# Layer entries reordered, an f16 projection in the fourth layer, and the adjacency's row sums on ScalarE

## The reference

```python
def reference(x, adj, ...):
    h = jnp.maximum(_layernorm(x, axis=-1), 0.0)
    x = x + _L0_gnn_ref(h, adj, L0_gnn_W, L0_gnn_a, L0_gnn_wtrans)   # attention, two softmaxes
    h = jnp.maximum(_layernorm(x, axis=-1), 0.0)
    x = x + _L1_gnn_ref(h, adj, L1_gnn_W, L1_gnn_b)    # relu(D^-1/2 adj D^-1/2 h W + b), D: row sums of adj
    h = jnp.maximum(_layernorm(x, axis=-1), 0.0)
    x = x + _L2_gnn_ref(h, adj, L2_gnn_weight)         # relu(adj (sign(h) sign(W)^T)), sign cut at 0
    h = jnp.maximum(_layernorm(x, axis=-1), 0.0)
    x = x + _L3_gnn_ref(h, adj, L3_gnn_t, L3_gnn_weight)  # s = h W: (1 - t) s + t adj s
    return x
```

## Time and profile before

| | us |
|---|---|
| median of 3 runs | 1005.76 (1004.84 to 1007.37) |
| profiled execution | 1004.67, its span 1003.0 |
| PE busy | 959.8 (96% of the span) |
| DVE busy | 761.0 (76%) |
| ACT busy | 442.5 (44%) |
| one-column matmuls, L1247 | 676 of them, 167 ns from start to end, overlapping their neighbours |
| adjacency load of 832 KB, issue to landing | 5.2 (median of 52) |

### The profile page before, as it was taken

How to read it: one execution, slowest core, us unless ns; L and a number is a source line. 1 busy time by engine, 2 the same in 40 slices (tenths; PEclk the granted TensorE clock), 3 DMA queues, 4 the chain that set the end, 5 groups by cost and what they waited for, 6 DMA issues and landing times.

```text
span 1003.0 us, 20390 instructions
## 1 busy us (share of the span) xinstructions
PE 959.8 (96%) x7677; PEld 710.9 (71%) x7677; DVE 761.0 (76%) x1141; ACT 442.5 (44%) x785; POOL 76.7 (8%) x156
## 2 busy tenths in 40 slices
PE   8889999999999999999999799999969999999995
PEld 8457788888888888888887345555758865555553
DVE  7688899999999999999997766655647765555553
ACT  6576677667777767777767311111100001111110
POOL 4100000000000000000030000000013320000000
PEclk9989999999999999999999899999989999999998
DMA  4803244343344424434015145554543455666561
GB/s 172 117 2 57 19 67 65 27 62 60 37 53 65 62 20 65 64 26 81 8 38 191 75 145 205 194 187 165 200 142 118 154 177 187 212 219 200 199 210 61
DMA packets 36423, 110.52 MB, mean 110 GB/s; under 512 B 4220, under 2 KB 24213, under 8 KB 36245
## 3 DMA queue, kind: packets, MB, share of 16 engines
q1 hardware_dynamic: 27653, 97.94, 28.2%
q0 software_dynamic: 7488, 11.08, 14.0%
q10 hardware_dynamic: 1232, 0.85, 0.3%
HBM read 128.58 MB, written 14.50 MB: 143 GB/s over the span
## 4 chain that ended last, share of the span: by engine, by line
PE 62%; DVE 21%; issue 9%; ACT 5%; DVEq 1%; DMA 1%; POOL 0%; ACTq 0%; POOLq 0%
PE f_ya L1413 15%; PE f_ya L1348 11%; PE f_ya L1244 10%; PE f_yb L1244 9%; PE f_ya L1399 6%; DVE f_wm L1596 6%; DVE f_gb L1597 4%; DVE f_s_mat L1602 4%; ACT f_gb L992 3%; PE f_yb L1234 2%; PE f_ya L1195 2%; PE f_yb L1319 2%; ACT f_s_mat L1002 2%; PE f_yb L1195 1%; PE f_ya L1150 1%
## 5 line engine op out<-in xcount | busy, mean ns | idle before, releaser
L1244 PE MATMUL f_ya<-f_x_mat,f_s_mat 128*128 128x257 f16 x2028 | 350.7, 272 | 1.9 <-DVE f_x_mat L1577 1.9
L1244 PE MATMUL f_yb<-f_x_mat,f_s_mat 128*128 128x257 f16 x2028 | 332.3, 273 | 0.0
L1244 PEld LDWEIGHTS f_yb<-f_x_mat,f_s_mat 128*128 128x128 f16 x2028 | 195.4, 96 | 27.1
L1244 PEld LDWEIGHTS f_ya<-f_x_mat,f_s_mat 128*128 128x128 f16 x2028 | 149.9, 97 | 19.1 <-issue 2.4
L1413 PE MATMUL f_ya<-f_x_mat,f_a 128*128 128x512 f16 x676 | 154.1, 379 | 0.0
L992 ACT ACTIVATE f_gb<-f_e_tile,f_expc 128x256 f32<-128x256 f32 x338 | 139.8, 493 | 0.0
L1002 ACT ACTIVATE f_s_mat<-f_wm 128x1792 f16<-128x1792 f32 (+1 forms) x52 | 82.7, 1590 | 114.5 <-DVE f_wm L1596 101.6
L1750 DVE SCALAR_TENSOR_TENSOR f_gb<-f_gb 128x1664 f32<-128x1664 f32 x52 | 97.8, 1891 | 35.2 <-DMA f_gb<-adj_dram 24.2
L1413 PEld LDWEIGHTS f_ya<-f_x_mat,f_a 128*128 128x128 fp8e4 x676 | 66.2, 98 | 71.8
L1247 PE MATMUL f_ya<-f_ones,f_a 128*128 128x1 f16 x676 | 112.9, 167 | 0.0
L1596 DVE TENSOR_TENSOR f_wm<-f_gb,f_a 128x1792 f32<-128x1792 f32 (+1 forms) x52 | 98.1, 1887 | 16.3 <-ACT f_gb L992 14.5
(11 more groups left out here) (165 smaller groups left out, 824.8 us busy)
## 6 DMA issues: line engine op xcount, KB each, us to landing
f_gb<-adj_dram SPq DMA_DIRECT2D x52, 832.0 KB, 5.2
f_a<-f_a_dram SPq DMA_DIRECT2D x32, 832.0 KB, 4.5
f_a<-adj_t_dram POOLq DMA_DIRECT2D x26, 224.0 KB, 4.9
f_a_dram<-f_a SPq DMA_DIRECT2D x26, 224.0 KB, 2.9
f_wm<-f_a_dram SPq DMA_DIRECT2D x7, 832.0 KB, 4.5
f_a<-adj_t_dram POOLq DMA_DIRECT2D x26, 192.0 KB, 4.8
f_a_dram<-f_a SPq DMA_DIRECT2D x26, 192.0 KB, 2.9
out_dram<-f_s_mat SPq DMA_DIRECT2D x25, 128.0 KB, 4.6
```

The costliest lines, as they stand in the source:

```text
L1244: return pe.matmul(bank[:, 0:F + 1], s_mat[:, j, side, i], x_mat[:, j, x_side, 0:F + 1], start=start, stop=stop)
```

## The change

1. **Row sums.** In all pairs but the last the one-column matmul goes. Instead GpSimd loads rows of `adj` (cast to fp8, `load_rows`, two buffers, two tiles a pair), ScalarE copies each half tile onto itself and accumulates its sum (`add_row`, 1664 elements, one per chunk, behind `products` of the next chunk), and VectorE adds the two halves (`add_rows`). The last pair still uses TensorE.
2. **First to second layer.** VectorE's and ScalarE's work on the last pair (`divisors`, `divide`, `whole`, `elu`, `row_sizes(2)`) stands behind `low1(4, 8)` and not behind `low1(16, 24)`. The range flags move from ahead of `low_sums(0)` to behind the four updates of group 0, and get two more (a third weight and `t`). The low half of w1 is made earlier.
3. **Second to third layer.** No checks stand behind group 5's updates; checks 21 to 24 stand behind group 6's. Pairs 2 and 3 of the adjacency are loaded early, into the buffer `wide[0]`.
4. **Third to fourth layer.** Four checks move from the fourth layer into the third, in two twos. The fourth layer takes its adjacency from four buffers (`slots3`) and its sums go to four banks in turn; the epilogues of tiles 0 and 1 stand within tiles 2 and 3.
5. **f16 projection.** The transposed sums are split into two f16 halves (ScalarE `turned_copy`, VectorE `low3`), and six f16 matmuls (two halves by two halves, without low times low) take the place of two f32 ones, which the trace shows as four.

The line numbers of the changed kernel differ: L1025 is `products`, L1035 and L1041 `high_minus` and `high_plus`, L1050 `add_row`, L1059 `divide`.

The diff, cut to its core:

```diff
+        slots3 = [wide[0][:, 1], wide[0][:, 0], a8[:, 1], a8[:, 0]]
...
-        EPILOGUE_AT = {3: (13, 19)}
+        EPILOGUE_AT = {3: (13, 20)}
         WEIGH_AT = (3, 4, 6, 8)
+        CHECK_AT = [range(4 * g + 1, 4 * g + 5) for g in range(GROUPS - 2)] + [range(0), range(4 * GROUPS - 7, CHECKS1)]
+        CHECK_LOADS = [range(4 * g + 2, 4 * g + 6) for g in range(GROUPS - 2)] + [range(4 * GROUPS - 6, 4 * GROUPS - 5), range(4 * GROUPS - 5, CHECKS1)]
...
+                    if g == GROUPS - 3:
+                        load_extra(2, 1)
...
+                for q in range(1, PAIRS):
+                    wait(mm_done[2], 2 * q + 2)
+                    if q == 1:
+                        load_pair(2, 4, 0)
+                        load_pair(2, 5, 1)
+                    elif q < 4:
+                        load_slot(q - 2)
+                    elif q < PAIRS - 2:
+                        load_pair(2, q + 2, q % 2)
+                    else:
+                        load_slot(q - PAIRS + 4)
+                    if q == 8:
                         load_check(13, 1, CHECKS1 + 2)
                         load_check(14, 0, CHECKS1 + 3)
...
+                def load_rows(t):
+
+                    if t > 1:
+                        g.wait_ge(rows_done, 2 * t - 2)
+                        g.sem_inc(waited, 1)
+                    g.dma_start(rows8[:, t % 2, :], io["adj"][t * P:(t + 1) * P, :]).then_inc(rows_here[t % 2], 16)
+
                 for m in range(PAIRS):
                     for c in range(NC):
                         load_a8(m, c)
+                        if m == 1 and c == NC - 1:
+                            load_rows(0)
+                        if m > 1 and c % 2 == 0:
+                            load_rows(2 * m - 3 + c // 2)
...
+                def add_row(m, r, c):
+
+                    p, half = c // 2, c % 2
+                    if half == 0:
+                        a.wait_ge(rows_here[p], 16 * m)
+                        settle()
+                    part_of = rows8[:, p, half * HW:(half + 1) * HW]
+                    a.activation(part_of, part_of, ACT.Copy, saturate=False, accum_out=row_parts[:, r, c:c + 1])\
+                     .then_inc(rows_done, 1)
...
+                        add_row(m, r, c)
...
-                x1_run(4, t)
+                x1_run(4, 8)
+                divide(PAIRS - 1, 0)
+                x1_run(8, 12)
+                for p in range(2):
+                    elu_exp(t + 2 + p, p)
+                x1_run(12, t)
...
-                    a.activation(yt_sb[:, 0:F], ep[:, 0:F], ACT.Copy).then_inc(zt_done[3], 1)
-
-                def pair(k, first):
+                    a.activation(zt16[:, 0], ep[:, 0:F], ACT.Copy, scale=Z3).then_inc(zt_hi, 1)
...
-                        pe.matmul(ya[s, p][:, F + 1:F + 2], a8[:, s, j, i], ones16[:, 0:1], start=False,
-                                  stop=(j == TILES - 1), skip_group_check=True)
+                        if last:
+                            pe.matmul(ya[s, p][:, F + 1:F + 2], a8[:, s, j, i], ones16[:, 0:1], start=False,
+                                      stop=(j == TILES - 1), skip_group_check=True)
...
+                        pe.wait_ge(zt_done[3], t + 1)
+                        for c in range(FB):
+                            for half, w_half in ((0, 0), (0, 1), (1, 0)):
+                                mm = pe.matmul(op[:, 0:F], zt16[:, half, c * P:(c + 1) * P], w3_16[:, w_half, c, :],
+                                               start=(c + half + w_half == 0), stop=(c == FB - 1 and half == 1))
+                        mm.then_inc(p_done[3], 1)
...
+                pair2(2, 0, 16, wide[0][:, 1], extra_here[1])
+                pair2(3, 1, 16, wide[0][:, 0], extra_here[0])
+                pair2(4, 0, 32, a8[:, 0], pair_here[2, 0])
...
+                LATE_AT = ({13: (2, 0, False), 20: (2, 1, True)},
+                           {3: (2, 0, False), 8: (2, 1, False), 15: (1, 0, False), 22: (1, 1, False)})
+                STEADY_AT = {EPILOGUE_AT[3][i]: (1, i, False) for i in range(2)}
+                for t in range(2, 10):
+                    q, p = t // 2, t % 2
+                    tile3(t, q % 4, 1 - q % 2, p, 16 * (q // 4) + 16, LATE_AT[p] if q == 1 else STEADY_AT)
...
+                def add_rows(m, r):
+
+                    v.wait_ge(rows_done, 4 * m)
+                    settle()
+                    v.tensor_tensor(rowsum[:, bass.ds(2 * m - 2, 2)], row_parts[:, r, 0:4:2], row_parts[:, r, 1:4:2], ALU.add)\
+                     .then_inc(row_added, 1)
...
-                        v.tensor_copy(rowsum[:, bass.ds(2 * m + p, 1)], ya[s, p][:, F + 1:F + 2]).then_inc(small, 1)
-                    v.wait_ge(small, 6 * m + 6)
+                        if isinstance(m, int) and m == PAIRS - 1:
+                            v.tensor_copy(rowsum[:, 2 * m + p:2 * m + p + 1], ya[s, p][:, F + 1:F + 2]).then_inc(small, 1)
+                    v.wait_ge(small, 4 * m + (6 if isinstance(m, int) and m == PAIRS - 1 else 4))
...
-                low1(4, 16)
+                low1(4, 8)
                 row_scales(1)
+                divisors(PAIRS - 1, 0)
+                for p in range(2):
+                    whole(t + 2 + p, 0, p)
+                low1(8, 12)
+                for p in range(2):
+                    elu(t + 2 + p, p)
+                row_sizes(2)
+                low1(12, 16)
+                row_scales(2)
+                low1(16, TILES)
                 v.wait_ge(late_w, 64)
+                v.wait_ge(w1_done, 1)
+                v.scalar_tensor_tensor(w1_16[:, 1], w_sb[1], WT, w1_16[:, 0], ALU.mult, ALU.subtract).then_inc(w1_done, 1)
                 w2v = w_sb[2]
                 step(v.tensor_scalar(scratch[:, 0], w2v, 0.0, None, ALU.is_gt))
                 step(v.tensor_scalar(scratch[:, 1], w2v, 0.0, None, ALU.is_lt))
                 v.tensor_tensor(sign_w, scratch[:, 0], scratch[:, 1], ALU.subtract).then_inc(signs, 1)
                 v.tensor_copy(ident16, ident[:]).then_inc(signs, 1)
-                low1(16, t + 2)
-                divisors(PAIRS - 1, 0)
-                for p in range(2):
-                    whole(t + 2 + p, 0, p)
-
-                for p in range(2):
-                    elu(t + 2 + p, p)
-                row_sizes(2)
-                row_scales(2)
-                low1(t + 2, t + 4)
...
+                    def low3(t):
+
+                        v.wait_ge(zt_hi, t + 1)
+                        v.scalar_tensor_tensor(zt16[:, 1], ep[:, 0:F], Z3, zt16[:, 0], ALU.mult, ALU.subtract)\
+                         .then_inc(zt_done[3], 1)
...
+                            if g == 0:
+                                range_flags()
+                            for n in CHECK_AT[g]:
...
+                        pairs(0, 3)
                         check(CHECKS1, 1)
                         check(CHECKS1 + 1, 0)
-                        pair(0, True)
-                        with v.Fori(1, PAIRS - 1) as k:
-                            pair(k, False)
-                        pair(PAIRS - 1, False, True)
+                        pairs(3, 5)
+                        check(CHECKS1 + 2, 1)
+                        check(CHECKS1 + 3, 0)
+                        pairs(5, 6)
```

278 lines of the change are left out of this document (153 added, 125 removed).

## The result

The changed kernel takes 994.51 us (median of 4 runs, 992.91 to 995.02), the kernel before 1006.26 in the same series. The ratio is 0.9885, with a 95% interval of 0.9871 to 0.9899: 1.15% less, some 11.6 us. The forecast was 997.6. The profiled execution of the changed kernel took 995.02 us with a span of 993.4, against 1004.67 and 1003.0: the traces account for 9.6 of the 11.6 us.

What follows compares the result with a forecast made beforehand. VectorE and ScalarE, at one pace with TensorE, were taken to bound the main loop. 0 - 2.7 - 4.6 - 4.2 + 3.4 = -8.1 us from 1004.67 gives 996.6, with 1.1 for the median 997.6 us; range 993 to 1001.5.

Steps and rivals of the forecast that it cites:

- Row sums: Main loop: VectorE and ScalarE set the pace, so removing 624 matmuls gains nothing; -1.1 to +1.3 us, taken as 0.
- a sign of being right: Main loop: its end was to come within 1.5 us of 542.4.
- the lead of 1.1 us that doesn't grow: Main loop, last pair's chunk 2: VectorE and ScalarE finish only 1.1 us before TensorE starts it.
- the rival of a TensorE bound: Main loop: producers have slack the trace hides, so the loop gives 16 us more; 981 us, chance 5%.
- First to second layer: Layer entry through group 2: first projection 7.0 us earlier, a new 4.3 us wait in group 2, net -2.7 us.
- The new wait of 4.3 us: Group 2: `low_sums(1)` ends at 601.9 behind flags and checks, while TensorE wants it at 597.6.
- Second to third to fourth layer: Group 5 to the fourth layer's tile 2: VectorE sets the third layer's pace; tile 2 starts earlier, -4.6 us.
- 22 tiles: Third layer: 22 tiles at VectorE's 2.70 us an update, plus four checks (7.3 us), put the last update at 816.3.
- Fourth layer: Fourth-layer tiles: f16 projection saves 0.22 us a tile, `low3` fits between transposes and projection; -4.2 us.
- Clock: Half clock behind new waits in group 2 and at the fourth layer's start: 1.7 us each, +3.4 us (0 to 7).
- The rival of long copies: Main loop: accumulating copies exceed the 2.05 us gap, each us over delaying 48 chunks; 1034 us at 2.8 us, chance 8%.

Runs made afterwards that it cites:

- flags, checks and products split: Changed kernel with range flags in four pieces between later checks, checks 21 and 22 behind group 5, two of the next chunk's products ahead of `high_minus`: 975.93 us, ratio 0.9706.
- copies twice: Changed kernel with a second accumulating copy of the same 1664 elements ahead of each of ScalarE's 48: 1019.27 us, ratio 1.0142.
- products split, sums on TensorE: Changed kernel with two of the next chunk's products ahead of `high_minus`, `divide` behind products, one-column matmuls back in all pairs, no ScalarE copies: 994.83 us, ratio 0.9888.

## Why the prediction was right

The time fell within the range, 3.1 us below the forecast, and the mechanism came out as told, with two terms mis-sized: the loop's and, less, the clock's.

**Row sums: no gain to speak of (step held, term mis-sized).** The forecast said that the producers set the pace, and that 18.7 us of matmuls turn into TensorE's idle time. The trace shows 11.7 us of it, and the run with the sums back on TensorE the same total time. The term was 0, with -1.1 us as its lower bound; the loop's end measured -2.4. That is outside the term's own range, and outside the 1.5 us that the text named as a sign of being right. 1.0 us is the lead that TensorE took (1.09 us at the last chunk 2 before, 0.15 now). The text named it and yet didn't put it into the sum. 0.8 us came in pair 0 (VectorE starts pair 1 at 105.60, not 106.41 us), where TensorE was the bound, which I hadn't looked at. 0.6 us are VectorE's 0.06 us a pair. The lead was also read at its smallest. In the kernel before it is 2.03 us at chunk 2 of pair 1, grows to 2.70 in pair 11 and falls to 1.09 in the last, where VectorE's turn takes 37.2 us. VectorE's other turns take 35.57 us on average against TensorE's 35.63, so TensorE was the slower by a hair, and the argument of "the lead of 1.1 us that doesn't grow" against the rival of a TensorE bound was weaker than it looked. The copies measured 1.57 us (1.6 taken).

**First to second layer (held).** Shifted by the loop's 2.4 us, block 12 starts within 0.1 us of the forecast 555.35, the first projection 0.5 us from 571.2, `low_sums(1)` ends 0.3 us from 601.9. Of the 7.0 us some 4 are the order's, by the run that undoes it. The new wait of 4.3 us is the flags': with them out of the way group 2 is 6.6 us shorter, which is the 4.03 us and the 2.6 us of half clock behind it. So the place of the flags gave back what this stretch had won.

**Second to third to fourth layer (held).** VectorE's first update, its even pace (2.72 us an update) and its two breaks for checks are there. On the forecast's time base the last update starts at 816.1 (816.3 forecast; its "22 tiles" should read 25 steps from the first update to the last, which is what gives 816.3). From group 3 to tile 2 the trace has -3.2 us, where -4.6 and 1.7 for the clock give -2.9. No run undoes this part (the order of the checks, the early loads, the four buffers) by itself, so its share rests on the traces and on what is left: 11.6 us less 4.6 for the entry and 4.2 for the projection leaves 2.8, uncertain by some 3 us. Splitting the checks won 8.2 us (7.1 by the ratios), which shows that the checks ahead of the first update were what TensorE waited for.

**Fourth layer (held).** -4.2 us forecast. By the trace -4.0, from tile 2 to the last matmul; by the run with the f32 projection 5.1 there and 4.3 with the end. The forecast's own terms (24 tiles at 5.60, 25 epilogues at 0.87 for 24 at 1.09) give 4.4 and not 4.2. Behind the last tile `low3` and the shorter projection were to cancel out; against the f32 projection they cost 0.8 us.

**Clock (held in kind).** +3.4 us taken. 20.5 us at half clock against 17.1. In group 2, 33.0 - 26.4 = 6.6 us are 4.0 of wait and 2.6 of clock, where I had 1.7. At the start of the fourth layer 1.7 us came as taken: from the last update to tile 2 it takes 10.26 us, and 8.57 in the run with flags, checks and products split, where the half clock had passed by then.

**The rival of long copies** was priced wrongly. It had each us above a gap cost one us from 2.05 us a copy on; the doubled copies showed that ScalarE's idle time counts over the pair, 4.46 us in all. By that a copy could have been some 1.57 + 1.1 = 2.7 us long before the loop became slower, an estimate that no run tested.

**The sum** lay 1.5 us above the traces' difference (8.1 against 9.6): 2.4 us from the loop and 0.3 from group 3 to tile 2, less 1.1 in groups 0 to 2 (0.9 of it the clock) and 0.2 in the fourth layer. The other 1.6 of the 3.1 us are luck of the executions: the forecast set the median 1.1 us above the profiled execution, as before, and after it lay 0.5 below.

## What to carry to other kernels

Where two sets of engines run at one pace, work taken from one of them buys only the lead; read that lead off the last chunk, put it into the sum, and look at the first turn by itself. Slack of an engine that trades waits with another is a sum over the whole turn, not the smallest gap. Work that is needed only at the end (flags, checks) belongs where its engine waits for something else anyway, in pieces: each of two such moves won more (7.4 and 8.2 us, 6.5 and 7.1 by the ratios) than any part of this change.

## What the runs showed of the hardware

Whether TensorE's clock falls behind a wait of 2.3 to 3.0 us differs between executions. Nine traces have such a wait at block 12 of the second layer's first group: in three the granted clock fell to 0.50 there (2.32, 2.67 and 3.01 us), in six it stayed at 1.00 (2.31 and 2.32 us in two each, 2.67, 3.01). A wait of 3.83 us (copies twice, group 0) left it at 1.00. With the twelve waits of 4.03 to 5.19 us in the first groups of that layer it fell each time, for 3.4 or 6.8 us. In the main loop all fourteen traces have one wait of 1.93 us at about 105 us; in one of them (products split, sums on TensorE) the clock fell 1.1 us behind it, for 3.4 us. The short waits of the loop did nothing: copies twice has 31.7 us of TensorE's idle time there, thirteen pieces of it over 1.5 us, at 1.00 throughout.

An accumulating fp8 copy on ScalarE holds the engine 1.57 us for 1664 elements, between its 1.39 us for 1536 and 1.59 us for 1792 elements of f32 (from start to start).
